# Expert gathers one place earlier in Pool's list, and the tokens' products four units later in TensorE's

## Chip, cores and metric

The kernel is one program on one core of one Trainium2 chip. The metric is the device time of one execution in microseconds; of several executions the median is taken. Trace times count from the first instruction of the profiled execution.

## What is computed

A decoder of two layers over x (4 x 512 tokens, 512 wide), everything in fp32. In layer 0 the third block is a mixture of experts:

```python
logits = xf @ w_cls.T; scores = softmax(logits)
_, topk_idx = top_k(scores + bias, 8)              # 32 routed experts and 32 that do nothing
buf[e, pos] = token rows sent to expert e          # 256 places per expert
gu = einsum('ech,ehf->ecf', buf, w_gate_up)        # 512 -> 2 x 256
g, u = split(gu); act = silu(g) * u
y = einsum('eci,eih->ech', act, w_down)            # 256 -> 512
out[token] = (sum over its 8 choices of w * y) * (1 + weight of the choices that do nothing)
```

Around it stand linear and softmax attention, the learned graph over the context, latent cross attention and a gated feed-forward block with a Walsh-Hadamard transform; the change touches none of these.

## The kernel before

The stages follow one another, each in its own block of per-engine lists; nothing of a stage starts before all engines are through with the one before. Every engine runs its list in order; semaphores join them. fp32 products are done as three products of a high and a low part (`split_mm`, L59 to L61): ACT makes the high part with a copy, DVE or Pool the low part by subtraction.

**`graph_and_router`** (L1543) finds the experts of each token. Its end is what the change touches. For the last of four batches TensorE runs `table(B - 1)` (L1855), products that tell which token sits in which place of which expert. DVE adds them up (L2147, `add_table`) and makes token numbers (`sum_tokens`, L2284, tile `gr_token_of`). TensorE moves these across partitions (`move_tokens`, L1864, bank 3 of PSUM), and DVE copies them to the integer tile `index` (`keep_index`, L2289), from which the gathers of the next stage take their addresses. Beside this the attention weights of layer 1 are turned and split in 16 late units (`late_units`; four matrices W_q, W_k, W_v, W_o, four units each): TensorE transposes a unit into one of four banks (`LATE_BANKS`, L1907), ACT makes the high part (L2016), DVE the low part (L2306) or, for W_o, a plain copy (L2303). `move_tokens` stands in TensorE's list ahead of unit 4, the first of W_k; `keep_index` in DVE's ahead of unit 8, the first of W_v.

**`experts`** (L2395) runs over 32 experts; buffers come in two, expert e uses number e % 2. For an expert:
- SP loads W_gate_up (`first_gu`, L2454, 1 MB) and W_down (`first_d`, L2455, 512 KB) into the raw buffers, when the low parts of expert e-2 (`gu_lo`, `d_lo`) are made.
- Pool gathers its 256 token rows (`gather`, L2644, two indirect DMAs, tile `ex_rows`), when the rows of expert e-2 have been transposed (`turned`); and it makes the low part of W_down (`split_d`, L2634), when ACT has made the high part (`d_hi`, L2560).
- TensorE transposes the rows (`turn`, L2504), ACT and DVE split them (`x_hi` L2564, `x_lo` L2589) and the gate/up weights (`gu_hi` L2556, `gu_lo` L2589). TensorE multiplies (`gate_up`), ACT and DVE make `h` (silu L2568, `hid` L2601, `h_hi` L2570, `h_lo` L2589), TensorE multiplies by W_down (`down`). ACT (L2576) and DVE (L2609) copy the result, SP stores it (L2460).

TensorE's list is written out by hand, in a loop of two slots per turn (L2537): transposes of expert e+2, gate and up of e+1, down of e. ACT's list: silu(e), h_hi(e), x_hi(e+2), gu_hi(e+2), y(e), d_hi(e+2). DVE's is alike and has one piece of the transform of W2 per expert (L2621); for these SP loads `w2T` and stores `w_mixed` four times. Pool's list before is gather(0), gather(1), split_d(0), split_d(1), gather(2), and then, for each e, gather(e+3) and split_d(e+2).

Of the kernel before, what the change touches and what calls it, by code (L numbers as in the profile page):

```python
# [1533 lines left out]
E_ROUTED, E_ALL, TOPK = 32, 64, 8  # L1534
# [8 lines left out]
def graph_and_router(nc, env, tag, x_in, x_out, ctx_in, wq, wk, gamma, w_cls, bias, normed, none_row, slots, index, weights, w1, w3, w2, hadamard, w13T, w2T, late_jobs, first_gu, first_d, shared_x, shared_rows, w_gate_up, w_down):  # L1543

    with semaphores(nc) as take, ExitStack() as ctx:
# [99 lines left out]
        LATE_BANKS = (4, 5, 6, 7)  # L1645
        late_units = [(j, c) for j in range(len(late_jobs)) for c in range(NC)]

        def late_bank(u):
            return ps[:, LATE_BANKS[u % len(LATE_BANKS)], :]
# [4 lines left out]
        def late_highs(u):  # L1654
            return sum(1 for j, _ in late_units[:u + 1] if late_jobs[j][2] is not None)
# [112 lines left out]
        def _(pe):  # L1768
# [79 lines left out]
            def table(b):  # L1848
                pe.wait_ge(logT_copied, b + 1)
                pe.wait_ge(blocks_set, b + 1)  # L1850
                pe.wait_ge(vector_rows, b + 1)
                for t in range(NT):
                    for g in range(GROUPS):
                        e = SIDE * g
                        mm = pe.matmul(ps[:, LOGT, g * P // 2:(g + 1) * P // 2], rows_hot[:, t, e:e + SIDE, :].rearrange("p e r -> p (e r)"),  # L1855
                                       block_hot[:, :, t, e:e + SIDE, :], start=t + g == 0, stop=t == NT - 1 and g == GROUPS - 1, skip_group_check=True)
                mm.then_inc(tabled, 1)

            def move_tokens():
                pe.wait_ge(index_step, 1)  # L1860
                by_side = token_of[:].rearrange("p g (t w) -> p w g t", w=SIDE)
                for h in range(SIDE):
                    for w in range(SIDE):
                        mm = pe.matmul(ps[ROW * w:ROW * (w + 1), MOVED, h * GROUPS * HALVES:(h + 1) * GROUPS * HALVES], env.ident[:, ROW * h:ROW * (h + 1)],  # L1864
                                       by_side[:, w], start=True, stop=True, skip_group_check=True)
                mm.then_inc(moved, 1)
# [31 lines left out]
            for u, (j, c) in enumerate(late_units):  # L1898
                if u == len(LATE_BANKS):
                    table(B - 1)  # L1900
                    move_tokens()
                if c == 0:
                    pe.wait_ge(late_in[j], 16)
                if u >= len(LATE_BANKS):
                    pe.wait_ge(late_done, u - len(LATE_BANKS) + 1)
                for t in range(NT):
                    mm = pe.transpose(late_bank(u)[:, t * P:(t + 1) * P], late_raw[j][:, t, c * P:(c + 1) * P], env.ident[:])  # L1907
                mm.then_inc(late_turned, 1)
# [110 lines left out]
        def _(dve):  # L2019
# [261 lines left out]
            def sum_tokens():  # L2281
                add_table(B - 1)
                dve.wait_ge(tab_added, SIDE * B)
                dve.scalar_tensor_tensor(out=token_of[:], in0=found[:, :, 1, :], scalar=float(P), in1=found[:, :, 0, :], op0=ALU.mult, op1=ALU.add  # L2284
                                         ).then_inc(index_step, 1)

            def keep_index():
                dve.wait_ge(moved, 1)
                dve.tensor_copy(index[:], ps[:, MOVED, 0:SLOTS // P]).then_inc(index_kept, 1)  # L2289
# [5 lines left out]
            for u, (j, c) in enumerate(late_units):  # L2295
                high, low = late_jobs[j][1:]
                if u == len(LATE_BANKS):
                    sum_tokens()
                if u == 2 * len(LATE_BANKS):
                    keep_index()  # L2300
                if low is None:
                    dve.wait_ge(late_turned, u + 1)
                    dve.tensor_copy(high[:, c, :], late_bank(u)).then_inc(late_done, 1)  # L2303
                else:
                    dve.wait_ge(late_high, late_highs(u))
                    dve.tensor_tensor(low[:, c, :], late_bank(u), high[:, c, :].bitcast(F32), ALU.subtract).then_inc(late_done, 1)  # L2306
# [88 lines left out]
def experts(nc, env, tag, normed, index, out_rows, w_gate_up, w_down, w2T, w2_mixed, raw_gu, raw_d, shared_x, shared_rows):  # L2395
# [6 lines left out]
    with semaphores(nc) as take, ExitStack() as ctx:  # L2402
# [145 lines left out]
        def flat(ap):  # L2548
            return ap.rearrange("p a b -> p (a b)")
# [80 lines left out]
        @block.gpsimd  # L2630
        def _(pool):
            def split_d(i, u):
                d_hi_done[u].wait(pool, i, 1)
                pool.tensor_tensor(flat(d_lo[:, u]), flat(raw_d[:, u]), flat(d_hi[:, u]).bitcast(F32), ALU.subtract  # L2634
                                   ).then_inc(d_lo_done[u].sem, 1)

            SIDE = 4

            def gather(e):
                i, u = e // 2, e % 2  # L2640
                turned[u].wait(pool, i, 0)
                for t in range(CT):
                    at = CT * (E_ROUTED // SIDE * (e % SIDE) + e // SIDE) + t
                    pool.indirect_dma_start(rows[:, u, t, :], None, normed, bass.IndirectOffsetOnAxis(index[:, at:at + 1], 0)).then_inc(rows_in[u].sem, 16)  # L2644

            gather(0)
            gather(1)
            split_d(0, 0)
            split_d(0, 1)
            gather(2)  # L2650
            for e in range(E_ROUTED):
                if e + 3 < E_ROUTED:
                    gather(e + 3)
                if e + 2 < E_ROUTED:
                    split_d(e // 2 + 1, e % 2)

# [352 lines left out]
```

## Time and profile before

| | us |
|---|---|
| median of 3 runs | 3100.27 |
| lowest and highest | 3097.53, 3104.15 |
| the profiled execution | 3097.72 |
| its span, first to last instruction | 3095.9 |

Of the span TensorE is busy 81%, DVE 60%, ACT 40%, Pool 27%; its mean granted clock is 0.893 of full speed (1 is 2.4 GHz). The expert stage runs from about 1145 to 1551 us, the end of the router stage before it from about 1129 to 1145. The busy share is an average over stages with different limits, so the rows further down are all from these two stretches. In a timeline row a releaser in brackets says how long the engine had been idle and what ended it.

### The profile page before, as it was taken

The numbers are of one execution on the slowest core, as the hardware profiler recorded it, in microseconds if no ns is written. First come the engines' busy times: TensorE is split into PE (matmuls) and PEld (weight loads), VectorE is DVE, ScalarE is ACT, GpSimd is POOL, SyncE is SP. The second block draws the span as 40 slices with busy tenths as digits, with TensorE's granted clock in tenths as the row PEclk, the third lists the DMA queues.
The fourth block names the chain that finished last, engine by engine and source line by source line (L and its number), as shares of the span: only waits on it lengthen the run. The fifth ranks groups of instructions, "written<-read, shape, count | busy, mean of one in ns | idle before, by whom it ended". The sixth has DMA issues, their size and how long they took to land. (4 is left out here: it accounts for less than half of the span.)

```text
span 3095.9 us, 35090 instructions
## 1 busy us (share of the span) xinstructions
PE 2499.3 (81%) x12822; PEld 1665.5 (54%) x12822; DVE 1864.9 (60%) x2959; ACT 1241.8 (40%) x1873; POOL 851.1 (27%) x1176
## 2 busy tenths in 40 slices
PE   5898989854443348888717999999999969999999
PEld 4454545322222237788704445545555537888887
DVE  3756566528999965555546777556555534444443
ACT  2443435328755534555402334334333323333332
POOL 2222223116556633434362343001111110000000
PEclk8999999975665679999858999999999979999999
DMA  3213221222213246776586656333433414001000
GB/s 120 58 42 82 49 75 46 69 66 87 94 45 112 89 170 208 248 240 240 178 190 162 150 157 158 91 93 97 120 93 83 103 68 171 17 25 41 1 28 14
DMA packets 186940, 323.55 MB, mean 105 GB/s; under 512 B 20450, under 2 KB 52066, under 8 KB 186788
## 3 DMA queue, kind: packets, MB, share of 16 engines
q1 hardware_dynamic: 168356, 270.44, 29.3%
q0 software_dynamic: 15360, 50.34, 6.1%
q8 instruction: 88, 1.44, 0.2%
q10 hardware_dynamic: 3072, 0.79, 0.1%
q14 instruction: 64, 0.52, 0.1%
HBM read 182.30 MB, written 62.92 MB: 79 GB/s over the span
## 5 line engine op out<-in xcount | busy, mean ns | idle before, releaser
L757 DVE TENSOR_REDUCE at_negmax<-at_ps 128x2 f32<-128x1024 f32 (+3 forms) x256 | 258.9, 1016 | 119.2 <-PE at_ps L523 63.7
L670 ACT ACTIVATE at_probs<-at_ps 128x1024 f32<-128x1024 f32 (+3 forms) x256 | 221.8, 866 | 270.6 <-PE at_ps L538 267.8
L1367 DVE TENSOR_REDUCE a_negmax<-a_ps 128x2 f32<-128x1024 f32 x128 | 155.1, 1216 | 138.8 <-PE a_ps L1120 138.2
L59 PE MATMUL ff_ps<-ff_xnT_hi,ff_s_hi 128*128 128x512 f32 x512 | 200.8, 392 | 5.1 <-DVE ff_xnT_lo L2876 5.1
L60 PE MATMUL ff_ps<-ff_xnT_lo,ff_s_hi 128*128 128x512 f32 x512 | 200.1, 391 | 0.0
L61 PE MATMUL ff_ps<-ff_xnT_hi,ff_s_lo 128*128 128x512 f32 x512 | 200.1, 391 | 0.0
L1945 ACT ACTIVATE gr_act_signs<-gr_signed,gr_test 128x512 bf16<-128x512 f32 x248 | 177.3, 717 | 42.5 <-POOL gr_test L2338 23.7
L538 PE MATMUL at_ps<-at_qk 98*128 98x512 f32 (+3 forms) x512 | 172.1, 418 | 21.1 <-DMA at_qk<-at_mrow 11.4
L2906 DVE TENSOR_TENSOR ff_hid<-ff_hid,ff_ps 128x512 f32<-128x512 f32 x64 | 44.0, 688 | 238.5 <-ACT ff_hid L2851 238.5
L1268 ACT ACTIVATE a_probs<-a_ps 128x1024 f32<-128x1024 f32 x128 | 130.9, 1024 | 135.9 <-PE a_ps L1138 135.3
L518 PE MATMUL at_ps<-at_qk 96*128 96x512 f32 (+3 forms) x512 | 162.4, 381 | 17.4 <-DVE at_xnT_lo L818 8.0
L538 PEld LDWEIGHTS at_ps<-at_qk 98*128 98x128 f32 x512 | 83.5, 194 | 163.3 <-issue 91.4
L2851 ACT ACTIVATE ff_hid<-ff_ps 128x512 f32<-128x512 f32 x64 | 38.3, 598 | 303.3 <-PE ff_ps L61 303.3
L59 PE MATMUL ex_ps<-ex_x_hi,ex_gu_hi 128*128 128x256 f32 x512 | 155.1, 303 | 0.0
L2634 POOL TENSOR_TENSOR ex_d_lo<-first_d,ex_d_hi 128x1024 fp32r<-128x1024 f32 x32 | 94.0, 2937 | 207.5 <-ACT ex_d_hi L2560 207.5
L60 PE MATMUL ex_ps<-ex_x_lo,ex_gu_hi 128*128 128x256 f32 x512 | 150.9, 295 | 0.0
L61 PE MATMUL ex_ps<-ex_x_hi,ex_gu_lo 128*128 128x256 f32 x512 | 150.1, 293 | 0.0
L852 POOL TENSOR_SCALAR_AFFINE_SELECT at_probs<-at_probs 128x256 f32<-128x256 f32 x128 | 52.7, 412 | 291.8 <-ACT at_probs L670 291.8
L782 DVE RECIPROCAL at_weighed<-at_weighed 128x128 f32<-128x128 f32 x128 | 119.7, 939 | 15.1 <-ACT at_weighed L705 15.1
L726 ACT CAST at_part<-at_ps 128x512 fp32r<-128x512 f32 x64 | 37.5, 587 | 211.9 <-PE at_ps L61 201.6
L873 POOL TENSOR_TENSOR at_oT<-at_weighed 128x512 f32<-128x512 f32 x32 | 40.8, 1274 | 296.2 <-DVE at_weighed L782 296.2
L630 PE MATMUL at_ps<-at_wo,at_oT 128*128 128x512 f32 x256 | 115.8, 606 | 6.8 <-POOL at_oT L873 6.6
(431 smaller groups left out, 6651.2 us busy)
## 6 DMA issues: line engine op xcount, KB each, us to landing
at_qk<-at_part SPq DMA_DIRECT2D x384, 128.0 KB, 2.4
first_gu<-in_L_ffn_w_gate_up_dram SPq DMA_DIRECT2D x32, 1024.0 KB, 5.5
a_qk<-a_part SPq DMA_DIRECT2D x192, 128.0 KB, 2.4
first_d<-in_L_ffn_w_down_dram SPq DMA_DIRECT2D x32, 512.0 KB, 7.9
out_rows<-ex_y SPq DMA_DIRECT2D x32, 512.0 KB, 2.8
gr_aside_raw<-in_L_ffn_W_dram SPq DMA_DIRECT2D x48, 256.0 KB, 3.1
w13T<-gr_aside_out SPq DMA_DIRECT2D x32, 256.0 KB, 3.2
shared_x<-x_after_cross SPq DMA_DIRECT2D x8, 1024.0 KB, 7.9
```

The source lines that it names most:

```text
L59: pe.matmul(out, lh, rh, start=start, stop=False, skip_group_check=True)
L60: pe.matmul(out, lh, rl, start=False, stop=False, skip_group_check=True)
L61: return pe.matmul(out, ll, rh, start=False, stop=stop, skip_group_check=True)
L518: mm = pe.matmul(bank(key, i, 0, n), qk[0:KROWS, g % STACKS, 0, j, t * P:(t + 1) * P], qk[0:KROWS, g % STACKS, 1, j, 0:n], start=True, sto ...
L538: mm = pe.matmul(bank(key, i, lo), qk[0:KROWS + 2, g % STACKS, 1, j, t * P:(t + 1) * P], qk[0:KROWS + 2, g % STACKS, 0, j, lo:S], start=Tr ...
L630: mm = pe.matmul(bank(key, i), oT[:, dc, t * P:(t + 1) * P], woT[:, dc, :], start=dc == 0, stop=dc == NC - 1, skip_group_check=True)
L670: act.activation(probs[:, t % 2, 2 * w:2 * w + 2, lo:S], banks(("kq", g, s), lo), ACT.Exp, scale=SCALE).then_inc(free(("kq", g, s)), 1)
L757: dve.reduce_max(negmax[:, g % 2, :].rearrange("p (j t) -> p j t", t=NT)[:, 2 * w:2 * w + 2, t], banks(("qk", g, s), 0, width(g, t)), AX.X ...
L782: dve.reciprocal(weighed[:, 1, t * P:(t + 1) * P], weighed[:, 1, t * P:(t + 1) * P]).then_inc(rec_done, 1)
L1268: act.activation(probs[:, t % 2, 2 * w:2 * w + 2, :], banks(("kq", g, s)), ACT.Exp, scale=SCALE).then_inc(free(("kq", g, s)), 1)
L1367: dve.reduce_max(negmax[:, g % 2, :].rearrange("p (j t) -> p j t", t=NT)[:, 2 * w:2 * w + 2, t], banks(("qk", g, s)), AX.X, negate=True).t ...
L1945: act.activation(act_signs[:, j, :], src, ACT.Sign, scale=-1.0, bias=against, accum_out=total[:, i, j:j + 1]).then_inc(counted_to[j], 1)
```

## The change

In Pool's list of the expert stage gather(3) moves up to gather(2), and each later gather one turn of the loop ahead: gather(e+4) now stands in front of split_d(e+2), where gather(e+3) stood. In the router's end `move_tokens` goes from late unit 4 to unit 8 in TensorE's list (`table(B - 1)` stays at 4), and `keep_index` from unit 8 to unit 12 in DVE's. No instruction is added or removed.

```diff
             for u, (j, c) in enumerate(late_units):
                 if u == len(LATE_BANKS):
                     table(B - 1)
+                if u == 2 * len(LATE_BANKS):
                     move_tokens()
...
                 if u == len(LATE_BANKS):
                     sum_tokens()
-                if u == 2 * len(LATE_BANKS):
+                if u == 3 * len(LATE_BANKS):
                     keep_index()
...
             split_d(0, 0)
             split_d(0, 1)
             gather(2)
+            gather(3)
             for e in range(E_ROUTED):
-                if e + 3 < E_ROUTED:
-                    gather(e + 3)
+                if e + 4 < E_ROUTED:
+                    gather(e + 4)
                 if e + 2 < E_ROUTED:
                     split_d(e // 2 + 1, e % 2)
```

## Rows read from the trace of the kernel before

**Rows 1.** Waits of TensorE, 1193 to 1504 us: in total, times, longest.
```profile
PE ex_ps L2504 <- DMA ex_rows<-normed,index: 44.0, 13, 3.8
```

**Rows 2.** Timeline of TensorE, slot starts: start us, us, instruction, idle time and releaser.
```profile
1180.62 1.04 PE L2504 MATMUL ex_ps<-ident,ex_rows 128*128 128x128 f32 x8
1181.41 0.36 PE L59 MATMUL ex_ps<-ex_x_hi,ex_gu_hi 128*128 128x256 f32 x1
...
1193.86 1.92 PE L2504 MATMUL ex_ps<-ident,ex_rows 128*128 128x128 f32 x8 [3.70 <-DMA ex_rows<-normed,index]
...
1204.86 1.03 PE L2504 MATMUL ex_ps<-ident,ex_rows 128*128 128x128 f32 x8
...
1217.70 1.88 PE L2504 MATMUL ex_ps<-ident,ex_rows 128*128 128x128 f32 x8 [3.30 <-DMA ex_rows<-normed,index]
...
1504.22 1.68 PE L2504 MATMUL ex_ps<-ident,ex_rows 128*128 128x128 f32 x8 [3.27 <-DMA ex_rows<-normed,index]
```

**Rows 3.** Timeline of Pool and of SP's queue, a pair of experts.
```profile
1191.32 2.90 POOL L2634 TENSOR_TENSOR ex_d_lo<-first_d,ex_d_hi 128x1024 fp32r<-128x1024 f32 x1 [3.77 <-ACT ex_d_hi L2560]
...
1194.30 0.37 SPq L2454 DMA_DIRECT2D first_gu<-in_L_ffn_w_gate_up_dram  x1
...
1206.18 2.97 POOL L2634 TENSOR_TENSOR ex_d_lo<-first_d,ex_d_hi 128x1024 fp32r<-128x1024 f32 x1 [9.60 <-ACT ex_d_hi L2560]
1209.31 1.23 POOL L2644 DMA_INDIRECT ex_rows<-normed,index  x1 [0.16 <-issue]
1210.85 0.95 POOL L2644 DMA_INDIRECT ex_rows<-normed,index  x1 [0.31 <-issue]
```

**Rows 4.** DMA, 1193.8 to 1504 us: queues with packets, MB, share; median us to landing.
```profile
q1 hardware_dynamic: 40210, 60.76, 57.6%
q0 software_dynamic: 4160, 13.63, 12.0%
q14 instruction: 2, 0.02, 0.0%
...
first_d<-in_L_ffn_w_down_dram SPq DMA_DIRECT2D x26, 512.0 KB, 7.8
...
ex_rows<-normed,index POOLq DMA_INDIRECT x52, 6.7
```

**Rows 5.** Stretches: window and its us; busy PE, PEld, DVE, ACT, POOL; PEclk, DMA share, GB/s.
```profile
1204.86:1214.24 9.38, 9.38 (x69) 8.70 (x67) 7.39 (x6) 5.47 (x6) 5.15 (x3) 1.00 0.54 185
1193.80:1217.70 23.90, 20.54 (x136) 19.17 (x137) 13.77 (x13) 12.42 (x13) 9.62 (x7) 0.93 0.61 219
```

**Rows 6.** Timeline of ACT and DVE, two slots of a pair.
```profile
1193.90 0.62 ACT L2570 CAST ex_h_hi<-ex_hid 128x512 fp32r<-128x512 f32 x1 [0.76 <-DVE ex_hid L2601]
...
1208.94 1.90 ACT L2556 CAST ex_gu_hi<-first_gu 128x2048 fp32r<-128x2048 f32 x1
...
1210.88 2.29 DVE L2589 TENSOR_TENSOR ex_gu_lo<-first_gu,ex_gu_hi 128x2048 fp32r<-128x2048 f32 x1
```

**Rows 7.** SP's timeline at the slowest weight load, and the us to its landing.
```profile
1385.69 1.43 SPq L2454 DMA_DIRECT2D first_gu<-in_L_ffn_w_gate_up_dram  x1
1387.17 0.83 SPq L2455 DMA_DIRECT2D first_d<-in_L_ffn_w_down_dram  x1
...
first_d<-in_L_ffn_w_down_dram SPq DMA_DIRECT2D x1, 512.0 KB, 11.0
```

**Rows 8.** Timeline of the router stage's end, and Pool's first gather.
```profile
1131.75 1.22 DVE L2147 TENSOR_TENSOR gr_found<-gr_found,gr_ps 32x128 f32<-32x128 f32 x4
...
1133.29 0.63 PE L1864 MATMUL gr_ps<-gr_token_of,ident 128*32 128x16 f32 x32 [2.35 <-DVE gr_token_of L2284]
...
1135.62 0.69 DVE L2306 TENSOR_TENSOR at_wk_lo<-gr_ps,at_wk_hi 128x512 fp32r<-128x512 f32 x1 [2.39 <-ACT at_wk_hi L2016]
...
1141.69 2.47 DVE L2303 COPY at_wo<-gr_ps 128x512 f32<-128x512 f32 x4
...
1146.38 1.26 POOL L2644 DMA_INDIRECT ex_rows<-normed,index  x1 [17.41 <-SPq L180]
```

## The prediction

> **What bounds the kernel now.** The program is a chain of stages on one core, so I read the stage that the edits touch and ask which wait ends last there. First the list of waits: between 1193 and 1504 us, nearly the whole expert stage, TensorE has one wait only, for `ex_rows`, the gathered tokens of an expert: 13 times, 44.0 us in all [rows 1]. Then TensorE's timeline, cut to the transposes of L2504 with which each slot begins. A slot is: transposes of expert e+2, gate and up of e+1, down of e. The starts 1193.86, 1204.86, 1217.70 show a wait before an even expert and none before an odd one [rows 2]. The pair period is (1504.22 - 1193.86)/13 = 23.87 us. Of that, the slot after the wait takes 11.00 us (1193.86 to 1204.86); the other is 9.38 us of work, read from the stretch 1204.86 to 1214.24, in which TensorE is busy throughout [rows 5]; 3.5 us are the wait.
>
> Why only even experts wait stands on Pool's timeline [rows 3]. The gather of 1209.31 belongs to an even expert. It stands behind the split of W_down that began at 1206.18, and that split waited 9.60 us for ACT's `d_hi`, which needs the end of an earlier down product. The gather itself needs only its row buffer, free since the transposes that began at 1193.86 and took 1.92 us [rows 2]: it could have gone some 13 us sooner. Its second half starts at 1210.85; a gather takes 6.7 us to land [rows 4], so 1217.55, and TensorE starts at 1217.70.
>
> The wait costs twice. The granted clock is 1.00 over the slot without a wait and 0.93 over a pair [rows 5]: after an idle stretch TensorE runs for a while at the lower of its two levels (1.2 GHz), and the same eight transposes take 1.92 us after a wait and 1.03 us without [rows 2]. That is 11.00 against 9.38 us.
>
> **Part 1, gathers one expert further ahead.** Nothing is added or removed: 64 gather instructions, two per expert, and 32 splits stay. gather(2) and gather(3) stand behind the first two splits as before, so the wait for expert 2 stays. In steady state gather(e+4) comes right behind the split of e+1, at slot start + 4.3 us. (Slot start 1190.00 is 1180.62 + 9.38; the split from 1191.32 took 2.90 and a load was issued at 1194.30, [rows 2, 3].) It ends 2.5 us later and lands by slot start + 13.5. The transposes that want it come 2 x 9.38 = 18.76 us after slot start: slack 5 us. The two row buffers allow it, since expert e+2 is transposed at the head of this very slot, before Pool gets there. The gathers' DMAs have Pool's queue to themselves and pass no other transfer there; SP's list is untouched.
>
> What is late next?
> (a) TensorE itself, 9.38 us per slot.
> (b) The low part of the gate/up weights. In the slot in which ACT also reloads its table, `h_hi` starts at 1193.90 for 0.62 us [rows 6]. `x_hi` then waited for the late transposes; now it can start at 1194.5, takes 0.9 us, then come `gu_hi` 1.90 and DVE's `gu_lo` 2.29 [rows 6]: 1199.6, slot start + 9.6. Gate and up want it 9.38 + 0.79 us after slot start (0.79 is 1181.41 - 1180.62, [rows 2]), 10.17. Cover left 0.5 us; without it each us costs a us per pair.
> (c) The weight loads, issued 4.3 us after slot start, `first_d` 0.4 later, 7.8 us to landing [rows 3, 4]: 12.5. In the slot without the table load ACT turns to `gu_hi` at 1208.94 [rows 6], 4.1 us after its start, so 9.38 + 4.1 = 13.5; there `gu_lo` has 1.7 us to spare. So a load may take 10.7 us before TensorE stalls. The worst one, behind a store of `w_mixed`, was issued at 1387.17 and took 11.0 us; its `first_gu` went at 1385.69 [rows 7], so its slot had started 4.3 us before that, at 1381.4, and the issue was 5.8 us after it; 5.8 + 11.0 + 1.9 + 2.3 = 21.0 against 18.76 + 0.79 = 19.55 wanted, 1.5 us of stall. There are three such stores; I charge 2 us for all.
> (d) The DMA engines: 57.6 + 12.0 = 69.6% busy over 311 us [rows 4], 16.6 us per pair against 18.76 after, 89%. They fit, closely. In the old pairs two loads are already 9.4 us apart (1194.30 is one slot behind its predecessor), so the denser beat has been run half of the time.
>
> Sum of part 1: the first even wait that goes, 1193.86 - 1190.00 = 3.9 us; 13 pairs x (23.87 - 18.76) = 66.4 us; the last slot, behind the wait of 1504.22, 11.00 - 9.38 = 1.6 us; less 2 for the stores: 69.9 us.
>
> **Part 2, the tokens' products four units later.** TensorE idles 2.35 us for `gr_token_of`, then runs 0.63 us of products, then the W_k transposes [rows 8]. After the change the W_k transposes fill the idle time. DVE's next late piece, at_wk_lo, started at 1135.62 after 2.39 us idle [rows 8]; it can start when DVE's own adds and its sum are done, about 0.3 us after 1131.75 + 1.22 = 1132.97. `keep_index` (one small copy) goes behind the W_v pieces, still in front of W_o. Behind it in DVE's list stands only W_o, 2.47 us from 1141.69, and the expert stage's first gather starts 2.2 us after that ends, at 1146.38 [rows 8]. So what DVE wins there the next stage wins. Bounds: 0 (if the later pieces set their own pace) and 3.0 us (2.35 + 0.63). I take 2.3, the row that is nearest being DVE's idle. Only SP waits for the index before the end of the stage.
>
> **Sum.** 69.9 + 2.3 = 72.2 us. The profiled execution took 3097.72 us (span 3095.9 and 1.8 around it), so its like after is 3025.5. The median of the runs is 2.55 us above that execution: 3028.
>
> **Rivals.** *Forecast*, 3028: 76%.
>
> *The loop's back edge* (8%). The wait falls once per turn of TensorE's loop (L2537), at its head. If a part of it were the fetch of the loop's first instructions, moving the gather would not bring that part. For: the period. Against: TensorE starts 0.15 us after the landing worked out above, and the instruction queue q14 brought 2 packets in 311 us and 13 turns [rows 4]. Hidden under the old wait, such a cost can be anything from 0 to the 3.5 us of the wait; in full it gives back 14 x (3.5 + 1.6) = 71 us, 3099; a fifth of it, with the clock kept up, 10 us, 3038. The Trainium skill (Runtime: NRT & Kernel Launch, "Instruction fetch mechanics") has it that a taken branch to a target outside the fetched pages stalls until that page is fetched. By that rule, with the head outside, the time would be this rival's; the two packets speak against it.
>
> *Bound by DMA* (10%). Denser traffic makes every load land like the worst [rows 7]: 1.5 us in each of 28 slots, 42 us, 3070. For: 89% busy. Against: the second load of each old pair.
>
> *The split held up by the gather, slower than before* (3%). Each gather now stands in front of a split whose end frees the raw W buffers for the next load. If Pool came to the gather only when `d_hi` is ready, loads would start 2.5 us later, and with loads of 11.0 us [rows 7] miss by 1.5 + 2.5 = 4 us per slot: 28 x 4 = 112, 3140. It decides when Pool's work per slot, 2.9 + 2.5 = 5.4 us [rows 3], reaches the slot's 9.38; it is 4 us short.
>
> *No effect* (3%): another wait of the same size takes the place, 3100.
>
> **How the numbers follow.** The forecast's own ends: no stall behind the stores, 3 us from part 2, a low run (2.7 us under the median as before): 3020 after rounding. At the other end 0.5 us missed in each of 14 table-load slots (7), nothing from part 2, and 3 to 4 us more of stalls and scatter: 3041. The mild ends of the back edge (3038) and of the DMA case fall inside 3020 to 3044, which leaves out two in ten. A difference of 0.2%, 6 us, is about what a measurement of this kernel can tell from none. Faster: 76 + 10 + most of 8 and a remainder, 0.95; within 0.02; slower 0.03.
>
> **What would show it.** Right: no wait for `ex_rows` in the steady stretch, slots of 9.4 us throughout at clock 1.00, Pool's gather 4.3 us after each slot start, the wait for expert 2 still there, W_k transposes straight behind the table's products. Wrong: a gap at every second slot with the gather landed long before (back edge); ACT's `gu_hi` waiting for a DMA (loads); splits that start well after `d_hi` ends (Pool).

## The result and the profile after

The changed kernel takes 3031.47 us (median of 4 runs, 3029.31 to 3036.53), the kernel before on the same chip 3100.81 us (3097.53 to 3104.15). The ratio is 0.9779, 95% interval 0.9762 to 0.9796. The forecast was 3028 us in a range of 3020 to 3044. The profiled execution took 3030.03 us, its span is 3028.2 us, its mean granted clock 0.900.

Waits of TensorE in the expert stage after the change (engine, tile, line, what was waited for; us in total, times, longest). The list answers to [rows 1]:

```profile
PE ex_ps L59 <- issue: 5.8, 8, 1.4
PE ex_ps L59 <- DVE ex_h_lo L2590: 3.9, 1, 3.9
```

The 44.0 us of waiting for `ex_rows` are gone. The 3.9 us belong to the last expert, and were there before. The eight gaps at L59 are new: small holes in front of a gate/up product, with no releaser that the profile could name. What they wait for is shown further down, under "What makes the second beat?".

TensorE's timeline, the starts of slots (start us, us, instruction). The first four answer to [rows 2]:

```profile
1174.37 1.04 PE L2505 MATMUL ex_ps<-ident,ex_rows 128*128 128x128 f32 x8
1183.76 1.03 PE L2505 MATMUL ex_ps<-ident,ex_rows 128*128 128x128 f32 x8
1193.13 1.03 PE L2505 MATMUL ex_ps<-ident,ex_rows 128*128 128x128 f32 x8
...
1305.65 1.03 PE L2505 MATMUL ex_ps<-ident,ex_rows 128*128 128x128 f32 x8
1315.03 1.03 PE L2505 MATMUL ex_ps<-ident,ex_rows 128*128 128x128 f32 x8
1316.70 0.36 PE L59 MATMUL ex_ps<-ex_x_hi,ex_gu_hi 128*128 128x256 f32 x1 [0.64 <-issue]
1325.29 1.03 PE L2505 MATMUL ex_ps<-ident,ex_rows 128*128 128x128 f32 x8
1334.99 1.03 PE L2505 MATMUL ex_ps<-ident,ex_rows 128*128 128x128 f32 x8
1336.50 0.36 PE L59 MATMUL ex_ps<-ex_x_hi,ex_gu_hi 128*128 128x256 f32 x1 [0.47 <-issue]
```

From 1174.37 to 1315.03 there are 15 slots of 9.38 us, the figure of the forecast. From 1315.03 on they last 10.26, 9.70, 10.09, 9.71 us and so on, 13 of them to the end. So the stage has two beats: one of 18.76 us per pair, and a longer one of some 19.8. Busy times in the two parts (window and its us; busy PE, PEld, DVE, ACT, POOL; PEclk, DMA share, GB/s):

```profile
1183.79:1315.03 131.24, 131.24 (x954) 123.65 (x952) 96.93 (x84) 86.58 (x91) 70.62 (x42) 1.00 0.88 303
1315.03:1433.18 118.15, 114.49 (x813) 105.65 (x812) 100.19 (x72) 72.17 (x77) 61.61 (x36) 1.00 0.85 289
```

The clock is 1.00 (2.4 GHz) in both, so the longer beat isn't the clock's doing; what stands out is DVE, busy 74% of the first part and 85% of the second with the same work per slot.

The end of the router stage, timeline of all engines (answers to [rows 8]):

```profile
1127.91 2.82 PE L1908 MATMUL gr_ps<-ident,gr_adjacent 128*128 128x128 f32 x16
1128.91 1.22 DVE L2148 TENSOR_TENSOR gr_found<-gr_found,gr_ps 32x128 f32<-32x128 f32 x4
...
1130.17 0.23 DVE L2285 SCALAR_TENSOR_TENSOR gr_token_of<-gr_found 128x64 f32<-128x64 f32 x1
1130.42 2.48 DVE L2307 TENSOR_TENSOR at_wk_lo<-gr_ps,at_wk_hi 128x512 fp32r<-128x512 f32 x4
1130.66 0.45 PE L1864 MATMUL gr_ps<-gr_token_of,ident 128*32 128x16 f32 x32
...
1135.35 2.47 DVE L2304 COPY at_wo<-gr_ps 128x512 f32<-128x512 f32 x4
1140.04 1.26 POOL L2645 DMA_INDIRECT ex_rows<-normed,index  x1 [13.91 <-SPq L180]
```

The W_k transposes run while DVE adds; the tokens' products wait for nothing; DVE goes from its sum into `at_wk_lo` with no wait that the profile lists.

**Where the time went.** I cut both traces at events that the change doesn't move. The stages ahead of the last choice's products (the first product of L1822 for the last batch) took 1109.2 us before and 1106.4 after; nothing was changed there, and in the other kernels below the same point lies between 1108.0 and 1117.1, so these 2.8 us are scatter. From there to the first gather it is 37.18 and 33.66: 3.5 us from the tokens' products. From the first gather to TensorE's last down product, which waits for `h_lo`, it is 390.74 and 328.90: 61.8 us from the gathers. What follows takes 0.5 us more. Sum 67.6 of the 67.7 by which the spans differ. Below, "the stage" is the stretch from first gather to last down product; it doesn't contain the scatter of the earlier stages, and is the sharper measure.

### The profile page after: what moved, and what is told of

It is laid out like the page before. It is cut to its first block and busy times, and to the rows that moved or that the text cites. A ratio compares the mean times of both kernels' runs of the same rounds, so it can differ in the third digit from the quotient of the medians.

```text
span 3028.2 us, 35090 instructions
## 1 busy us (share of the span) xinstructions
PE 2476.7 (82%) x12822; PEld 1644.7 (54%) x12822; DVE 1884.0 (62%) x2959; ACT 1239.5 (41%) x1873; POOL 851.9 (28%) x1176
## 3 DMA queue, kind: packets, MB, share of 16 engines
q8 instruction: 88, 1.44, 0.2%
## 5 line engine op out<-in xcount | busy, mean ns | idle before, releaser
L59 PE MATMUL ff_ps<-ff_xnT_hi,ff_s_hi 128*128 128x512 f32 x512 | 200.8, 392 | 5.1 <-DVE ff_xnT_lo L2878 5.1
L59 PE MATMUL ex_ps<-ex_x_hi,ex_gu_hi 128*128 128x256 f32 x512 | 148.4, 290 | 6.3 <-issue 5.8
L2635 POOL TENSOR_TENSOR ex_d_lo<-first_d,ex_d_hi 128x1024 fp32r<-128x1024 f32 x32 | 87.4, 2730 | 136.5 <-ACT ex_d_hi L2561 136.4
```

The source lines that it names most:

```text
L59: pe.matmul(out, lh, rh, start=start, stop=False, skip_group_check=True)
```

## Experiments

### Each part alone

`gathers_only` has the change in Pool's list alone; `tokens_only` that of `move_tokens` and `keep_index` alone.

> The change's first part alone (move_tokens at late unit 4 and keep_index at unit 8, as before). Between the last choice products of the router and the first gather, the kernel before took 37.2 us and the changed one 33.5 us, so part 2 seems worth 3.5 us. If the parts are independent: about 3035 us, ratio 0.979, with the expert stage as in the changed kernel: slots of 9.38 us, and where the second pattern sets in, pairs of 19.8 us. By the prediction's own term for part 2 (2.3 us) it would be 3034. If part 2 were worth nothing: 3031.5.

> The second part alone, gathers as before. Expected 3.5 us under the kernel before, 3097 us, ratio 0.999, with the pair period of the expert stage still 23.9 us and DVE's last copy of W_o 3.5 us earlier after the table's products. By the prediction's term 2.3 us; if the router's end is not what starts the expert stage, 3101.

Measured: `gathers_only` 3036.44 us, ratio 0.9802 (0.9786 to 0.9819); stage 326.73, router's end 37.17. `tokens_only` 3096.49 us, ratio 0.9995 (0.9982 to 1.0009); stage 390.70, router's end 33.65. Each stretch moves with its own part and not with the other: 64.0 us and 3.5 us. The second is below what the runs' times can show and is clear only in the trace. In `gathers_only` the longer beat sets in too, only later, with the slot of 1362.28.

### Is a part of the wait bound to the loop's head?

```diff
-                if e + 4 < E_ROUTED:
+                if e + 4 < E_ROUTED and e % 2 == 0:
                     gather(e + 4)
                 if e + 2 < E_ROUTED:
                     split_d(e // 2 + 1, e % 2)
+                if e + 4 < E_ROUTED and e % 2 == 1:
+                    gather(e + 4)
```

> As the changed kernel, but only the gathers of even experts stand in front of the split, those of odd experts behind it as before. Theory (a gather behind the split of its slot is issued 4.3 us into the slot before it is wanted, and lands 3.5 to 4 us after the 9.4 us slot is over, for whichever expert): the wait moves from the even experts to the odd ones, pair period again 23.9 us, time about 3097 us, ratio 0.999, TensorE's waits for ex_rows in the middle of its loop body and none at its head. Rival 1 (the loop's back edge): the wait stays at the head of the loop. Rival 2 (only even experts' gathers were late): nothing of the gain is lost, about 3031 us, ratio 0.978.

Measured: 3090.44 us, ratio 0.9978 (0.9968 to 0.9989), stage 388.57. That is some 8 us under the kernel before in the same series, where 3.5 had been expected from part 2 alone; the stage gives 2.2 of the rest, and what is left, some 2 us, no row explains. Waits of TensorE over the stage, and its timeline at the first of them:

```profile
PE ex_ps L2505 <- DMA ex_rows<-normed,index: 44.7, 13, 5.2
```

```profile
1201.82 1.09 PE L2505 MATMUL ex_ps<-ident,ex_rows 128*128 128x128 f32 x8 [3.06 <-DMA ex_rows<-normed,index]
1212.75 1.03 PE L2505 MATMUL ex_ps<-ident,ex_rows 128*128 128x128 f32 x8
```

There are 13 waits again, now at 1201.82, 1225.83, 1249.33 and so on: these are odd experts, in the middle of the loop's body. At the head, where all waits of [rows 1] stood, this stretch has none left. So the wait follows the place of the gather and not the branch. It also shows that the change is worth little by halves: as long as one gather of a pair stands behind its split, a pair takes about as long as before (on average 23.7 us from 1201.82 to 1510.25).

### What makes the second beat?

The trace after shows how it begins. Timeline of SP's queue, ACT, DVE and Pool around the onset; a piece of the transform of W2 is L2622:

```profile
1297.66 0.46 SPq L2466 DMA_DIRECT2D shared_rows<-w2T  x1
...
1301.06 3.27 SPq L2456 DMA_DIRECT2D first_d<-in_L_ffn_w_down_dram  x1
...
1312.37 1.91 ACT L2557 CAST ex_gu_hi<-first_gu 128x2048 fp32r<-128x2048 f32 x1 [2.53 <-DMA first_d<-in_L_ffn_w_down_dram]
...
1314.31 2.29 DVE L2590 TENSOR_TENSOR ex_gu_lo<-first_gu,ex_gu_hi 128x2048 fp32r<-128x2048 f32 x1 [2.69 <-ACT ex_gu_hi L2557]
...
1316.37 2.49 POOL L2635 TENSOR_TENSOR ex_d_lo<-first_d,ex_d_hi 128x1024 fp32r<-128x1024 f32 x1 [3.79 <-ACT ex_d_hi L2561]
1316.52 0.68 DVE L2610 COPY ex_y<-ex_ps 128x512 f32<-128x512 f32 x1
1317.12 2.81 DVE L2622 TENSOR_TENSOR shared_x<-shared_x 128x1024 f32<-128x1024 f32 x1
```

The same two instructions in the short beat, where the piece of the transform comes first:

```profile
1203.32 1.22 DVE L2622 TENSOR_TENSOR shared_x<-shared_x 128x1024 f32<-128x1024 f32 x1
...
1203.85 2.95 POOL L2635 TENSOR_TENSOR ex_d_lo<-first_d,ex_d_hi 128x1024 fp32r<-128x1024 f32 x1 [3.80 <-ACT ex_d_hi L2561]
```

The load of `first_d` behind the 1 MB load of `w2T` takes 3.27 us to issue alone and lands late; ACT's `gu_hi` waits for both weight loads, which count on one semaphore, so `gu_hi` and `gu_lo` run late, and DVE comes to its piece after Pool has begun the split. Then the piece ends at 1319.93, 1.1 us after the split's end (1318.86), and takes 2.81 us in place of 1.22. Had the piece come first, the split would have paid: the piece ends at 1204.54, and the split at 1206.80, 2.26 us later, where a split that starts first takes 2.40. The Trainium skill ("SBUF — State Buffer", "Who interferes with whom") has this as a rule: a DVE instruction with two inputs in SBUF contends with a GpSimd instruction that reads SBUF, the port pair that they share is an exclusive lock, and the order in which they are issued decides which of them is held up. Both pairs of rows agree to within 0.15 us: each time the second ends 0.14 or 0.15 us before the end of the first plus its own unblocked time.

*My theory*: the 1.6 us that DVE loses make its next `hid`, `h_hi`, `gu_lo` late, so that its next piece comes after the split again; one late load is enough for the rest of the stage. One slot of the trace after shows this ring (DVE and ACT, from one `gu_lo` to the next):

```profile
1334.11 2.29 DVE L2590 TENSOR_TENSOR ex_gu_lo<-first_gu,ex_gu_hi 128x2048 fp32r<-128x2048 f32 x1 [0.58 <-ACT ex_gu_hi L2557]
1336.92 2.88 DVE L2622 TENSOR_TENSOR shared_x<-shared_rows 128x1024 f32<-128x1024 f32 x1
1339.73 0.68 DVE L2602 TENSOR_TENSOR ex_hid<-shared_rows,ex_ps 128x512 f32<-128x512 f32 x1
1340.44 0.62 ACT L2571 CAST ex_h_hi<-ex_hid 128x512 fp32r<-128x512 f32 x1 [2.27 <-DVE ex_hid L2602]
1341.87 1.91 ACT L2557 CAST ex_gu_hi<-first_gu 128x2048 fp32r<-128x2048 f32 x1
1343.81 2.29 DVE L2590 TENSOR_TENSOR ex_gu_lo<-first_gu,ex_gu_hi 128x2048 fp32r<-128x2048 f32 x1 [0.58 <-ACT ex_gu_hi L2557]
```

`gu_lo` ends at 1336.40 and again at 1346.10, 9.70 us later, and TensorE's gate/up products start 0.10 us behind each end (1336.50 and 1346.20). So the gaps marked "issue" are waits for `gu_lo`, and in the longer beat this ring sets the length of a slot, and no longer TensorE's own work. The products start 1.51 and 1.12 us behind the starts of their slots, 0.79 in the short beat: 0.72 + 0.33 = 1.05 us, by which a pair is longer. The ring has 1.66 us in it that the blocked piece costs; without them it would close in about 8.1 us (an estimate from these rows and the end of silu at 1338.16), under the slot's 9.38. And the order keeps itself: the split comes some 1.3 us behind each slot start, the piece some 0.5 us behind the end of `gu_lo`, so a `gu_lo` that ends more than some 0.8 us behind the slot start lets the split go first (an estimate from these rows); here it ends 1.41 and 1.02 us behind it.

*Rival*: the denser traffic makes loads late again and again. Against it speaks already that in the trace after ACT waits for a load once (0.71 us, at 1432.21) in the 13 long slots. Three kernels tell them apart. `small_fly` cuts the piece to 8 columns of one row block (so it leaves out the transform but for these), `small_w2` cuts the transfers of `w2T` and `w_mixed` inside the stage to a sixteenth and keeps the pieces (it leaves out most of W2's data, and stores three full tiles ahead of the loop), and `late_once` keeps all transfers and makes `gu_lo` late one single time:

```diff
                     split_x(i + 1, u)
+                    if (i, u) == (2, 0):
+                        gu_hi_done[u].wait(dve, i + 1, 1)
+                        for k in (slice(0, 1024), slice(1024, 1280)):
+                            dve.tensor_tensor(spare[:, k], flat(raw_gu[:, u])[:, k], flat(raw_gu[:, u])[:, k], ALU.add)
                     split_gu(i + 1, u)
```

> As the changed kernel, but each of DVE's 32 steps of the W2 transform works on 8 elements per partition instead of 1024 (the transform is left out but for these), all waits and transfers kept. In the changed kernel, from 1315 us on, slots run 10.1 and 9.7 us instead of 9.38. Theory A (order of DVE and Pool: once a low part of the gate/up weights is late, DVE's step of the transform starts after Pool's split and takes 2.8 to 3.3 us instead of 1.2, which makes the next low part late again): slots of 9.38 us from first to last, 7 to 8 us faster than the changed kernel, about 3024 us, ratio 0.975. Theory B (DMA: the weights land late because the traffic is dense): the gaps stay, since the traffic is the same: 3031 us, ratio 0.978.

> As the changed kernel, but the loads of w2T (the three in the loop and the first) and the three stores of w_mixed in the loop move 64 KB instead of 1 MB; the transform works on what lies in the tile, and three full tiles are stored before the loop, so part of the W2 data is left out. DVE's steps keep their length. Theory A says such a transfer only sets off the slow pattern, by making one weight load land late, and DVE against Pool keeps it going: without them it isn't set off, slots of 9.38 us to the end, about 3024 us, ratio 0.975. Theory B (dense traffic) gives the same sign: 3024 too; the two are told apart by the run with the short steps and by the one with a single delay. If the slow pattern comes by itself from the 0.5 us of cover, it is there: 3031 us.

> As the changed kernel, but DVE does two useless additions (1024 and 256 elements per partition, about 1.6 us together) once, in front of the low part of the gate/up weights of expert 6. Theory A (the slow pattern keeps itself going): from there on, at about 1222 us, every pair takes 19.8 instead of 18.76 us, so the slow pattern has 12 pairs instead of 7: 5 us more than the changed kernel, about 3037 us, ratio 0.980. Theory B (each gap has its own late load) and any theory without memory: one gap of about 1.2 us, then slots of 9.38 again until 1315 us: 3033 us.

Measured: `small_fly` 3025.75 us, ratio 0.9771 (0.9748 to 0.9794), stage 319.22; `small_w2` 3030.98 us, ratio 0.979 (0.9771 to 0.9809), stage 319.65; `late_once` 3040.08 us, ratio 0.9822 (0.98 to 0.9843), stage 333.38. Waits of TensorE in front of gate/up, from 1185 to 1450 us, of `small_fly` and then of `late_once`; in `small_w2` the list is empty:

```profile
PE ex_ps L59 <- issue: 1.2, 1, 1.2
```

```profile
PE ex_ps L59 <- issue: 6.0, 12, 0.8
```

In `small_fly` a load is late (ACT waits 3.25 us for it at 1359.28, behind the store of `w_mixed` at 1344.01), one slot takes 10.82 us, and the next are 9.38 again: a late load by itself costs 1.44 us and leaves nothing behind. In `small_w2` ACT waits 0.2 us for a load in all, and the 28 slots are all 9.37 or 9.38. Its median is that of the changed kernel all the same, 7 us above the 3024 expected, although its stage is 9.3 us shorter. In its profiled execution (span 3028.2) the unchanged stages ahead of the router's end came out 10.4 us longer than in the trace after; whether they did in its other executions no trace shows, so this stays open. Its second slot was 1.4 us longer, beside the three full stores, which SP issued in 9.80 us from 1159.93 on. So I let the stage decide between the theories, and not the run times of these kernels. `late_once` settles it: the added 1.56 us are spent once, at 1212.13, and after a first slot of 10.37 the pairs of 10.1 and 9.7 run from there to the end, without a single wait of ACT for a DMA. Its rows at the onset, Pool first and DVE behind it, as above:

```profile
1215.54 2.60 POOL L2640 TENSOR_TENSOR ex_d_lo<-first_d,ex_d_hi 128x1024 fp32r<-128x1024 f32 x1 [4.06 <-ACT ex_d_hi L2562]
...
1216.40 2.82 DVE L2627 TENSOR_TENSOR shared_x<-shared_x 128x1024 f32<-128x1024 f32 x1
```

and over all pieces from 1216 on (window and its us; DVE busy in this line and its count; PEclk, DMA share, GB/s), 73.99 / 24 = 3.08 us for each:

```profile
1216.00:1452.00 236.00, 73.99 (x24) 1.00 0.86 292
```

### The changed kernel again

> The changed kernel once more, profiled a second time, to see whether the second slot pattern (10.1 and 9.7 us in turn instead of 9.38) sets in again and where. Theory (one weight load that lands late puts DVE's piece of the W2 transform behind Pool's split, and the lag then keeps itself alive): slots of 9.38 us until the slot after one of the transfers of w2T or w_mixed, from there pairs of about 10.1 and 9.7 to the end of the stage, so the onset may differ between executions but lies behind such a transfer. A pattern that starts at once at a place with no such transfer, or that ends by itself, speaks against. Rival (no memory: each gap is a late load of its own): single gaps scattered over the stage, with 9.38 between. Time about 3031 us by both.

Measured: 3033.35 us (3025.99 to 3038.56), ratio 0.9782 (0.9758 to 0.9807), stage 332.98. The short beat lasts only seven slots here, until 1245.18, then the pairs of 10.1 and 9.7 go on to the end. The onset is the same chain, behind another load of `w2T`:

```profile
1227.81 0.46 SPq L2466 DMA_DIRECT2D shared_rows<-w2T  x1
1230.79 1.49 SPq L2455 DMA_DIRECT2D first_gu<-in_L_ffn_w_gate_up_dram  x1
1232.33 2.26 SPq L2456 DMA_DIRECT2D first_d<-in_L_ffn_w_down_dram  x1
```

```profile
1242.38 1.91 ACT L2557 CAST ex_gu_hi<-first_gu 128x2048 fp32r<-128x2048 f32 x1 [2.38 <-DMA first_d<-in_L_ffn_w_down_dram]
```

```profile
1246.52 2.40 POOL L2635 TENSOR_TENSOR ex_d_lo<-first_d,ex_d_hi 128x1024 fp32r<-128x1024 f32 x1 [3.78 <-ACT ex_d_hi L2561]
```

```profile
1247.13 2.87 DVE L2622 TENSOR_TENSOR shared_x<-shared_x 128x1024 f32<-128x1024 f32 x1
```

Over three traces (after, after again, gathers alone) the long beat began at 1315, 1245 and 1362 us and never ended by itself. Which transfer starts it differs between executions, a load of `w2T` in two of them and a store of `w_mixed` in the third; stages of 326.7 to 333.0 us are what comes of that. ACT had waited 2.53, 2.38 and 3.09 us for the load that started it. Three shorter waits for a load, of 1.51 us in the trace after and of 1.37 and 0.72 in `gathers_only`, had come before and lengthened no slot: small delays are covered.

### Versions that avoid it

`fly_first` puts the piece of the transform (`between` in the diff) ahead of the copy of `y` in DVE's list, so that a late `gu_lo` has the copy's 0.7 us in hand before Pool's split is met. `both` adds the gather of expert 2 ahead of the second split, the wait that the change left at 1162.98 (4.55 us). `spread` adds to both that each later load of `w2T` goes as four quarters in four slots and each store of `w_mixed` as two halves.

```diff
                     split_gu(i + 1, u)
+                between()
                 y_ready[u].wait(dve, i, 2)
...
             split_d(0, 0)
+            gather(2)
             split_d(0, 1)
-            gather(2)
             gather(3)
...
-                if i % STAGES == 2:
-                    load_w2(i // STAGES + 1)
+                if i % STAGES in (1, 2) and i // STAGES + 1 < NT:
+                    load_w2(i // STAGES + 1, 2 * (i % STAGES - 1) + 1)
```

> As the changed kernel, but DVE's step of the W2 transform stands in front of its copy of y instead of behind it, so that it starts as soon as the low part of the gate/up weights is done. Theory A: in the fast pattern it then runs before Pool's split; a low part has to be 0.6 us later than now before the order turns. The slow pattern is rarer or absent: 3024 to 3031 us, ratio 0.975 to 0.978. If the step in that place delays y or the next h by more than there is cover for, slots are longer than 9.38 us from the start and it is slower than the changed kernel: up to 15 x 1.2 us, 3049.

> As the run before it, and gather(2) stands between the first two splits instead of behind them. Its rows then land while TensorE does the gate and up of expert 0, and the wait of 4.55 us for expert 2 goes, with 1.6 us of lower clock behind it: 6 us less than the run before it, about 3018 to 3025 us, ratio 0.974. Rival: the split of expert 1, now 2.5 us later, delays the second weight load and through it the stage by as much as is won: no difference.

> As the run named both (transform piece ahead of the copy of y in DVE's list, gather of expert 2 ahead of the second split), and each later load of w2T goes out as four transfers of a quarter in four slots instead of one, each store of w_mixed as two halves in two slots. Theory: what is left of late loads comes from those large transfers in SP's queue; no load lands late, every slot is 9.38 us, the stage takes about 311 us (both: 312.84) and the time is about 2 us under that of both, 3018 us, ratio 0.975. Rival: the weight loads are late by the density of the traffic itself, or the added transfers cost queue time of their own; then gaps of the same size are found at other slots and the stage is no shorter than 312.8, time 3020 or above.

Measured: `fly_first` 3027.45 us, ratio 0.9771 (0.9755 to 0.9787), stage 320.08; `both` 3019.8 us, ratio 0.9755 (0.9739 to 0.9771), stage 312.84; `spread` 3014.15 us (3011.02 to 3020.23), ratio 0.9728 (0.9703 to 0.9752), stage 310.82. The waits of TensorE, `fly_first` from 1185 to 1450 us:

```profile
PE ex_ps L59 <- issue: 1.6, 2, 1.1
```

and `spread` from 1150 to 1455 us, the whole stage behind its first wait:

```profile
PE ex_ps L59 <- DVE ex_h_lo L2597: 2.8, 1, 2.8
PE ex_ps L2512 <- DVE ex_x_lo L2597: 2.5, 1, 2.5
```

In `fly_first` ACT waits 3.1 us for a load at 1361.24 and the next piece meets the split (3.42 us at 1365.40, the split at 1364.74); slots of 10.91 and 10.07 us follow each other. But then the order turns back, piece at 1375.63 and split at 1375.66, and the beat with it: the earlier place in the list doesn't prevent the first blocking, it ends it. DVE and Pool in the slot in which the order turned back:

```profile
1375.63 1.22 DVE L2623 TENSOR_TENSOR shared_x<-shared_x 128x1024 f32<-128x1024 f32 x1
1375.66 3.45 POOL L2635 TENSOR_TENSOR ex_d_lo<-first_d,ex_d_hi 128x1024 fp32r<-128x1024 f32 x1 [4.76 <-ACT ex_d_hi L2561]
```

`both` does the same (10.38 and 10.05, then 9.38) and its stage is 7.2 us shorter again, which is the second wait and the slot at the lower clock behind it (its eight transposes take 1.96 us in `fly_first`, 1.03 in `both`). In `spread` no gap is left; ACT has no wait for a DMA in the stage, and all slots from the third on are 9.37 or 9.38. The DMA share meanwhile is the highest of all, 0.90 of 246 us:

```profile
1184.00:1430.00 246.00, 31.66 (x26) 1.00 0.90 306
```

(same columns; 31.66 / 26 = 1.22 us for a piece, never blocked). So in these traces neither the mean load on the DMA engines nor the number of transfers makes a load late, but a single 1 MB transfer in front of it; of `spread` there is one trace. It has the lowest median of this study. Its interval and that of the changed kernel (0.9758 to 0.9807 in the same series) don't overlap; with that of `both` (0.9739 to 0.9771, another series) it does, so only the trace says that the quarters and halves add something.

## Why the prediction was right, step by step

- **What bounds.** Right. Without the late gather the waits are gone, and the slot is TensorE's own work at clock 1.00.
- **Size of a pair.** Right: 28 slots take 334.58 us before and 262.55 us in `small_w2`, where nothing disturbs them; 72.0 us, and the forecast's terms without the charge for stores give 66.4 + 3.9 + 1.6 = 71.9.
- **Pool's gather** at slot start + 4.3: 1197.56 - 1193.13 = 4.4. The wait for expert 2 stays, 4.55 us.
- **(b), `gu_lo` in the slot with the table load**, forecast to end at slot start + 9.6 with 0.5 us of cover: it starts at 1303.57 for 2.29 us in the slot of 1296.28, which is 9.58.
- **(c), late loads: the term that was mis-sized.** I charged 2 us for three stores of `w_mixed`. What one late load costs directly was about right (1.5 us forecast, 0.9 in the slot of 1315.03, 1.4 in `small_fly`). (The cover was 0.1 to 0.2 us larger than I wrote: 19.55 - 13.5 - 4.2 is 1.9 and not 1.7.) Missed was, first, that the loads of `w2T` do it as well, and second, what a late load leaves behind. In the trace after, the 28 slots take 270.75 against 262.55 us, and the stretch after the last slot's start 23.82 against 21.93: 10.1 us in place of 2. I had followed TensorE, ACT and SP through a late load, but not asked what DVE's shifted piece would meet on Pool: in (b) and (c) DVE's work beside `gu_lo` stood at nothing. Of the signs that I had named, "slots of 9.4 us throughout" failed from 1315 on, and `gu_hi` waiting for a DMA, a sign against, came three times (1.51, 2.53 and 0.71 us). In the trace before the order was never in question: each piece started some 0.5 us ahead of its split (1215.04 and 1215.56, 1229.53 and 1230.04), and the 26 pieces from 1193.8 to 1504.2 took 31.59 us, 1.22 each.
- **(d), DMA.** Right: share 0.88 in the short beat, 0.89 forecast, and the kernel isn't bound by it; `spread` runs faster at 0.90.
- **Part 2: too low, and above its bound.** 3.5 us, where I took 2.3 of at most 3.0. The gap between DVE's adds and `at_wk_lo` went as worked out: 2.65 us before (1132.97 to 1135.62 [rows 8]), 0.29 after. But from the start of `at_wk_lo` to that of `at_wo` it was 6.07 us before and is 4.93 after: W_k's pieces, made to wait by late transposes before, now run back to back. 2.36 + 1.14 = 3.50. The upper bound lacked that term: of pieces behind the moved one I had counted the gap only, not the pace.
- **Sum.** The span forecast was 3023.7, measured 3028.2. 8.1 us more for the long beat, 1.2 less for part 2, 2.8 less from the scatter of earlier stages, 0.5 more behind the stage: 4.6 of 4.5.
- **Rivals.** The loop's back edge falls by `even_only` and by the heads of the loop without a gap in the trace after, in agreement with the two instruction packets of [rows 4]. Bound by DMA falls by `small_w2` against `spread`: 0.80 and 0.90 of share with the same 28 slots. The split held up by the gather: SP's load still goes at slot start + 4.4 (1197.49), it didn't happen. My forecast held in its main mechanism; that it came out within 4 us is partly luck, since an error of 8 us and two of 1 and 3 us stood against each other. The range's lower end was also worked out wrongly: 3028 - 2 - 0.7 - 2.7 is 3022.6; 3020 comes out only from 3025.5, which already lies 2.55 us under the median. The measured time lies above both.

Left open: why a load behind the same 1 MB transfer is late in one execution and in time in the next. SP's own issue of `first_d` took 3.27 us (1301.06) or 2.26 us (1232.33) in the two traces of the changed kernel where it started the long beat, and 0.50 as a rule. But a long issue doesn't tell a late load: in `gathers_only` it took 1.13 us where ACT then waited 3.09, and in the trace after 1.39 us at 1340.93, behind one of 2.09 for `first_gu`, where ACT waited for nothing. What sets this was not tried.

## What to carry to other kernels

When a wait goes, follow each step that will run later than planned, also on engines with time to spare, and ask for each instruction that would change its order against another engine's. A schedule that holds only as long as two instructions start in one order isn't settled by a mean load: one late transfer can turn it for the rest of the stage. Split the rare large transfers into pieces no larger than the regular ones, and put the instruction that can be blocked where it has slack on the side of the one that blocks it.

## What the hardware showed that I had not expected

- A DVE add over two SBUF inputs (128x1024) takes 1.22 us alone and 2.8 to 3.4 us when Pool's subtraction (2.40 us alone) has begun less than a microsecond before it; in the other order Pool's takes 2.95 us, and 3.45 where it begins 0.03 us behind.
- The stage has two beats that both keep themselves going, 18.76 and 19.8 us per pair, with the same instructions, the same clock and nearly the same DMA share (0.88 and 0.85).
- DMA engines busy 90% (306 GB/s) over 246 us held up no slot (one trace), while at 0.88 a 1 MB transfer in front of an expert's weight loads did.
